# Output projection of the scan stage: half rows of 256 columns over eight e-tiles in place of whole rows over four

## The reference

```python
def _L3_cond_ref(x, c, ...):              # S=512, D=512, E=1024, N=16, R=64
    def _ssm(u, Wdbc, Wdt, bdt, Alog, Dp):
        dlt, Bm, Cm = split(u @ Wdbc.T)
        delta = softplus(dlt @ Wdt.T + bdt)
        dA, dBu = exp(delta * A), delta * Bm * u
        h = dA_t * h + dBu_t              # a scan over time, for each e and each of N=16 states
        y = sum_n h * C_t
        return y + u * Dp
    z1 = _ssm(mz @ Wc1.T + bc1, ...)                  # first direction
    z2 = flip(_ssm(flip(mz @ Wc2.T + bc2), ...))      # second direction
    out = einsum('bse,de->bsd', act_mx * z1 + act_mx * z2, Wf) + bf + skip
    return x + gate[:, None, :] * out
```

## Time and profile before

| | us |
|---|---|
| median of 3 runs | 6557.69 |
| lowest, highest | 6544.21, 6568.91 |
| profiled execution | 6555.72 |
| its span | 6553.9 |
| the scan stage in it | from about 3450 to the end |

### The profile page before, as it was taken

One profiled execution on the slowest core, in us unless ns is written; L12 is line 12 of the kernel. 1 busy time (PEld: TensorE's weight loads), 2 busy tenths in 40 slices (PEclk: granted clock), 3 DMA queues, 4 the chain that ended last, 5 costly groups with the idle time before them and its releaser, 6 DMA issues. The chain is left out here.

```text
span 6553.9 us, 129603 instructions
## 1 busy us (share of the span) xinstructions
PE 5787.2 (88%) x54624; PEld 3049.2 (47%) x54624; DVE 4470.7 (68%) x6093; ACT 2749.7 (42%) x4645; POOL 2867.4 (44%) x921
## 2 busy tenths in 40 slices
PE   8899979996878777885988999999999999999998
PEld 2455545553444444442444545555454554545454
DVE  1265545554555565556628989989898998989886
ACT  0022212222333333331116666666566665656564
POOL 0010000000000000002326888888788887878886
PEclk9999989998988888887999999999999999999999
DMA  5200010101000000002431111111011111111110
GB/s 197 73 29 29 21 69 29 36 20 62 15 16 15 1 15 15 7 7 80 151 138 47 52 60 50 58 53 54 30 50 61 50 58 52 49 36 50 60 40 26
DMA packets 143104, 321.75 MB, mean 49 GB/s; under 512 B 25786, under 2 KB 27195, under 8 KB 132299
## 3 DMA queue, kind: packets, MB, share of 16 engines
q1 hardware_dynamic: 142546, 313.72, 13.9%
HBM read 238.79 MB, written 74.89 MB: 48 GB/s over the span
## 5 line engine op out<-in xcount | busy, mean ns | idle before, releaser
L1379 POOL TENSOR_TENSOR sc_state<-sc_state,sc_c_rows 128x2048 f32<-128x2048 f32 x512 | 2327.0, 4552 | 515.9 <-DVE sc_state L1663 512.3
L1663 DVE TENSOR_TENSOR_SCAN sc_state<-sc_decay,wide 128x512 f32<-128x512 f32 x2048 | 2342.9, 1202 | 285.6 <-PE wide L1533 285.3
L1462 ACT ACTIVATE sc_decay<-sc_delta,sc_neg_a 128x512 f32<-128x512 f32 x2048 | 1431.7, 717 | 1000.7 <-DVE sc_state L1663 1000.7
L1533 PEld LDWEIGHTS wide<-sc_diag,sc_du_t 64*64 64x64 f32 x32768 | 934.2, 133 | 682.0 <-DVE sc_state L1663 377.1
L1550 PE MATMUL wide<-sc_state,sc_half 64*64 64x512 f32 x8192 | 1080.6, 607 | 152.2 <-issue 140.7
L1533 PE MATMUL wide<-sc_diag,sc_du_t 64*64 64x128 f32 x32768 | 1123.1, 274 | 29.6 <-DVE sc_state L1663 25.6
L639 POOL TENSOR_SCALAR l_y_rstd<-l_y_mv 128x4 f32<-128x4 f32 x24 | 5.6, 234 | 1511.6 <-DVE l_y_mv L805 1511.6
L520 ACT ACTIVATE l_prob<-l_prob,l_s_max 128x512 f32<-128x512 f32 x512 | 363.2, 710 | 722.1 <-DVE l_s_max L536 722.0
L484 PE MATMUL wide<-l_ident,l_prob 128*128 128x128 f32 x2048 | 374.7, 338 | 266.7 <-DVE l_prob_t L553 266.3
L460 PE MATMUL wide<-l_w,l_xn_t 128*128 128x512 f32 x1280 | 556.3, 592 | 2.1 <-PEq L84 2.1
L1507 PE MATMUL wide<-sc_xn_t,sc_w_z 128*128 128x512 f32 x1024 | 508.9, 620 | 0.0
(11 more groups left out here) (171 smaller groups left out, 5953.4 us busy)
## 6 DMA issues: line engine op xcount, KB each, us to landing
sc_c_rows<-c_d SPq DMA_DIRECT2D x64, 1024.0 KB, 4.8
sc_w_z<-wz_tiles SPq DMA_DIRECT2D x128, 256.0 KB, 2.7
x<-l_out SPq DMA_DIRECT2D x24, 1024.0 KB, 4.9
l_x<-x SPq DMA_DIRECT2D x16, 1024.0 KB, 7.1
mx_d<-fr_mx SPq DMA_DIRECT2D x16, 1024.0 KB, 4.2
sc_mx<-mx_d SPq DMA_DIRECT2D x64, 256.0 KB, 2.6
pro_w_mod<-in_mod_w SPq DMA_DIRECT2D x6, 2048.0 KB, 8.4
l_w<-in_att_w SPq DMA_DIRECT2D x12, 1024.0 KB, 13.2
```

The source lines that it names most:

```text
L1379: pool.tensor_tensor(state[quad % STATES][:, :, :], state[quad % STATES][:, :, :], c_rows[(r * 4 + q) % ROWS][:, :, :], ALU.mult).then_inc ...
L1462: act.activation(decay[step % DECAYS][:, :], delta[slot % 2][:, :], ACT.Exp, scale=neg_a[:, s, m, n:n + 1]).then_inc(decay_ready, 1)
L1533: last = pe.matmul(to[cols_to, k, :, :], du_t[slot % 2][rows, k, cols_to], diag[rows, c, k, :, :], start=True, stop=True)
L1663: dve.tensor_tensor_scan(state[quad % STATES][:, step % 4, order], decay[step % DECAYS][:, order], pair[:, i, order], 0.0, ALU.mult, ALU.a ...
```

## The change

A row of 128 x 512 is made as two pieces of 128 x 256, each with all eight k, in the left half of `z_bank`. Piece 0 to 7 of a sequence are made in the slots at place 1 to 8, so in seven e-tiles of the first direction and the first of the second. Each of these slots has eight matmuls (two in each of the chunks 4 to 7) of 256 columns. VectorE drains each piece by itself into its half of `o_gated`, at places 2 to 9. GpSimd adds the residual once per row as before, at places 3, 5, 7 and 9 in place of 2 to 5. SyncE stores at places 4, 6, 8 and 10 in place of 3 to 6. `o_full` and `o_drained` count pieces now.

```diff
-                    if q == 1 and s == 0 and b >= 1 and 2 <= m <= 5:
-                        output(b - 1, m - 2)
+                    if q == 1 and b >= 1 and slot % 16 in (3, 5, 7, 9):
+                        output(b - 1, (slot % 16 - 3) // 2)
...
-                        if s == 0 and b >= 1 and m >= 3:
-                            pe.wait_ge(o_drained, (b - 1) * TT + min(m - 2, TT))
+                        if b >= 1 and slot % 16 >= 3:
+                            pe.wait_ge(o_drained, (b - 1) * 2 * TT + min(slot % 16 - 2, 2 * TT))
...
-                def output(b, t, ks):
+                def output(b, piece, ks):
+                    t, h = piece // 2, piece % 2
                     if 0 in ks:
                         pe.wait_ge(gated_ready, (b + 1) * ET)
-                        pe.wait_ge(o_drained, b * TT + t)
+                        pe.wait_ge(o_drained, b * 2 * TT + piece)
                     for k in ks:
-                        last = pe.matmul(z_bank, gated[:, k, t * P:(t + 1) * P], w_out[:, k, :],
-                                         start=(k == 0), stop=(k == ET - 1))
+                        last = pe.matmul(z_bank[:, 0:256], gated[:, k, t * P:(t + 1) * P],
+                                         w_out[:, k, h * 256:(h + 1) * 256], start=(k == 0), stop=(k == ET - 1))
...
-                    if 1 <= b < B and s == 0 and 1 <= m <= 4 and c >= 4:
+                    if 1 <= b < B and 1 <= slot % 16 <= 8 and c >= 4:
...
-                for t in range(TT):
-                    output(B - 1, t, range(ET))
+                for piece in range(2 * TT):
+                    output(B - 1, piece, range(ET))
...
-                    dve.tensor_tensor(o_gated[:, :], z_bank, gate[:, :], ALU.mult).then_inc(o_drained, 1)
+                    dve.tensor_tensor(o_gated[:, h], z_bank[:, 0:256], gate[:, h], ALU.mult).then_inc(o_drained, 1)
...
-                    if c == 0 and b >= 1 and s == 0 and 2 <= m <= 5:
-                        output(b - 1, m - 2)
+                    if c == 0 and b >= 1 and 2 <= slot % 16 <= 9:
+                        output(b - 1, slot % 16 - 2)
```

More of the change, by code:

```diff
@@ L1303, in _ @@
                         load_xn(b + 1)
-                    if s == 0 and b >= 1:
-                        o = b - 1
-                        if m == 0:
+                    if b >= 1:
+                        o, at = b - 1, slot % 16
+                        if at == 0:
                             load_gate(o)
[L1308 to L1319, removed]
+                        if at in (4, 6, 8, 10):
+                            store(o, at // 2 - 2)
+                        if at in (0, 2, 4, 6):
+                            t = at // 2
+                            if o * TT + t >= 2:
+                                sp.wait_ge(out_stored[t % 2], (o * 2 + t // 2) * 16)
+                            load_resid(o, t)
                     if m == 7 and r + 1 < 2 * B:
@@ L1323, in _ @@
                             load_c(4 * (r + 1) + q)
-                sp.wait_ge(o_drained, (B - 1) * TT)
+                sp.wait_ge(o_drained, (B - 1) * 2 * TT)
                 load_gate(B - 1)
@@ L1358, in gating @@
                     if m == 0 and b >= 1:
-                        pool.wait_ge(o_full, b * TT)
+                        pool.wait_ge(o_full, b * 2 * TT)
                     pool.tensor_tensor(gated[:, m, :], y_sum[:, m, :], mx[m % 2][:, :], ALU.mult
@@ L1363, in output @@
                 def output(b, t):
-                    pool.wait_ge(o_drained, b * TT + t + 1)
+                    pool.wait_ge(o_drained, 2 * (b * TT + t + 1))
                     pool.wait_ge(resid_loaded[t % 2], (b * 2 + t // 2 + 1) * 16)
@@ L1593, in _ @@
                             pe.wait_ge(z_direct, slot + 2)
-                        output(b - 1, m - 1, range(2 * c - 8, 2 * c - 6))
-                for t in range(TT):
-                    output(B - 1, t, range(ET))
+                        output(b - 1, slot % 16 - 1, range(2 * c - 8, 2 * c - 6))
+                for piece in range(2 * TT):
+                    output(B - 1, piece, range(ET))
             @block.vector
@@ L1642, in add_swapped, with output @@
                     dve.tensor_tensor(y_sum[:, m, :], s_bank, y_sum[:, m, :], ALU.add).then_inc(y_added, 1)
-                def output(b, t):
-                    if t == 0:
+                def output(b, piece):
+                    t, h = piece // 2, slice(piece % 2 * 256, (piece % 2 + 1) * 256)
+                    if piece == 0:
                         dve.wait_ge(gate_loaded, (b + 1) * 16)
-                    dve.wait_ge(o_full, b * TT + t + 1)
+                    dve.wait_ge(o_full, b * 2 * TT + piece + 1)
                     if b * TT + t >= 1:
                         dve.wait_ge(out_ready, b * TT + t)
-                    dve.tensor_tensor(o_gated[:, :], z_bank, gate[:, :], ALU.mult).then_inc(o_drained, 1)
+                    dve.tensor_tensor(o_gated[:, h], z_bank[:, 0:256], gate[:, h], ALU.mult).then_inc(o_drained, 1)
                 def scans(chunk):
@@ L1680, in _ @@
                         add_swapped(slot - 1)
-                    if c == 0 and b >= 1 and s == 0 and 2 <= m <= 5:
-                        output(b - 1, m - 2)
+                    if c == 0 and b >= 1 and 2 <= slot % 16 <= 9:
+                        output(b - 1, slot % 16 - 2)
                 add_sums(SLOTS - 1)
                 add_swapped(SLOTS - 1)
-                for t in range(TT):
-                    output(B - 1, t)
+                for piece in range(2 * TT):
+                    output(B - 1, piece)
 def program(nc, d, out):
```

## The result

| | before | after |
|---|---|---|
| median, us | 6553.46 (20 runs) | 6578.50 (20 runs) |
| lowest to highest | 6525.22 to 6575.27 | 6562.47 to 6592.03 |
| profiled execution, its span | 6555.72, 6553.9 | 6589.83, 6587.9 |

Ratio 1.0044, 95% interval 1.0031 to 1.0057: slower by 25 us by the medians and 29 by the ratio, close to what was forecast (6577), and within the 0.5% that was called no change. The interval goes from 20 to 37 us, so the ratio alone can't test the terms of the sum.

What follows compares the result with a forecast made beforehand. PE bounds the scan stage; output work costs PE time in full beyond a free 3.41 us behind `turn`. From 6555.72: +25.7 loop, +2.2 end, -6.8 clock, or +21.1, gives 6577 us, range 6553 to 6606.

Steps and rivals of the forecast that it cites:

- Part 1 and 2: PE at places 1 to 8: slots of 25.58 us, eight taking 204.98 against 201.31; +25.7 us over seven sequences.
- The switch of 0.36 us: PE going from quarters to full array and back, paid per chunk with output work in chunks 5 to 7: 0.36 us.
- the line and both bounds: Other estimates for a 256-column PE instruction: 0.225 us on a straight line between bounds of 0.120 and 0.435.
- the room behind `turn`: Stretch from `turn` to the first `sums`: fixed length, PE work in it free up to about 3.4 us.
- The 0.14 us "absorbed somewhere": In slots with output before: costs summed to 28.30 us, 28.14 was measured; the difference was also taken off the new slot.
- Part 3: End of the program: a row as two pieces takes 8.54 us against 7.98, +2.2 us for four rows.
- Parts 4 and 5: VectorE's added drains (+0.5 us a sequence) and GpSimd's and SyncE's moved additions and stores: cost nothing.
- Part 6: Half-clock stretches in second-direction slots: two places a sequence now carry output, so four stretches of 1.70 us fewer, -6.8 us.
- A: Rival: PE's gaps in eight slots swallow work and switches, 23.93 us a slot, 6489 us in all; chance 0.05.
- B: Rival: the clock falls in slots with output work, idle before chunk 5's `sums`: +25 us, 6602; chance 0.15.
- C: Rival: GpSimd becomes late at place 7 and PE waits 2.3 us a sequence: +16 us, 6593; chance 0.08.
- D: Rival: PE weight loads stand open behind short matmuls, 60 us in the loop and 14 at the end: 6652; chance 0.02.

Runs made afterwards that it cites:

- filled pair: Kernel before and changed kernel, each with unread 512-column matmuls behind `turn` in second-direction gaps without output work: medians 6525.64 and 6555.45 us.
- first filled kernel: Kernel before plus two unread 512-column matmuls behind `turn` in second-direction slots, from place 8 on: ratio 0.9969.
- narrow kernel: Kernel before with rows made as two 256-column halves in the same four slots: ratio 1.0023, or 0.9974 with unread matmuls in second-direction gaps.

## Why the prediction was right

- *Part 1 and 2, the loop.* 25.58 us a slot and 204.98 for the eight were forecast; 25.58 and 205.00 are in the trace, and the filled pair gives 26.4 us for the loop against 25.7. The switch of 0.36 us was worked out as a remainder and has since been measured alone (26.30 - 25.58 = 2 x 0.36). The 0.2155 us of a 256-column instruction is the 0.215 taken, and the 0.225 of the line and both bounds weren't needed. That the room behind `turn` doesn't move is seen in the 3.42 us; of it PE idled 0.77 us, a little less than the 0.8 to 1.0 forecast. The 0.14 us "absorbed somewhere" was carried over from the kernel before without a reason, and it held: of the three bare chunks only the first two take 1.74 and 1.73 us, and the third takes 4376.84 - 4374.99 = 1.85, so there output work adds 0.12 us less than the sum had.
- *Part 3, the end.* 8.60 us a row, 8.54 forecast: +2.5 by the rows at full clock and by the filled pair's traces, 2.2 forecast. VectorE's 256 columns took 0.42 us there (0.41).
- *Parts 4 and 5.* VectorE, GpSimd and SyncE cost nothing visible, as taken. SyncE's loads of the residual rows moved too, to places 0, 2, 4 and 6 in place of 0, 1, 3 and 4, which the prediction didn't weigh; no slot is longer for it.
- *Part 6, the clock, had no ground.* I took off 6.8 us because two susceptible slots a sequence now carry output. Those slots were indeed spared, but stretches came in others: 16 in the profile against 17, so 1.7 us in this pair, and single profiles scatter from 3 to 29. Filling the gap took 0.34% from the kernel before and 0.31% from the changed one, 22 and 20 us, so the credit is 2 us by this, with intervals that hold both 0 and 6.8. The unfilled means of 20 runs each, 6550.7 and 6579.8, differ by 29.1, with some 8 us either way, and don't decide it either. It also named the places 8 and 9; the two that count are 7 and 8, as the first filled kernel showed.
- The forecast of 6577 is nearer to 6578.5 than its working deserves: the profiled execution from which it started lay 2.3 us above the median of 20 runs, and it took off 6.8 us of clock where the two profiles differ by 1.7. With neither it would have been 6553.5 + 27.9 = 6581.4, which is inside the runs' scatter too. So the match to 1.5 us is in part luck; that of the slots is not.
- *Rivals.* A (gaps swallow the work) is excluded by the chunk of 2.95 us; the experiment with all matmuls in chunk 4 shows what it would have needed, work put where the gap is. B (the clock falls in slots with output) didn't come in any profile of the series. C and D are excluded by GpSimd's timeline and by the narrow kernel: its 448 added loads of the full array cost 0.9 us in the loop, and only the first step of a run is longer. The Trainium skill ("TensorE: Matmul & The Clock Gate", section "The mechanism") says that a weight load overlaps running matmuls only in other rows of the array; by that sentence alone the added loads would have stood open, and they didn't. The same section of the Trainium skill also has loads pulled ahead when they go to the background weight buffer. The prediction passed over this, and the 0.9 us agree with it.

What stays open: why some gaps of 1.44 us are followed by a half-clock stretch and others aren't. Slots at places 0 to 6 have the same gap of 1.44 us, with 0.12 us of idle ahead in place of 0.29, and had none. The prediction's range was right, but its assumption on the number of stretches had no mechanism behind it.

## What to carry to other kernels

Spreading work over more steps to fill idle time pays only if it is put where the idle time is: here the same instructions cost 205 us for eight slots spread over four chunks and 192 in one. Before you split a run of matmuls, subtract a bare step from one that holds the run; what its columns don't explain is paid again with each new run. And where PE must wait anyway, free work in the gap can be worth its place for the clock alone: here 0.3%.

## What was not expected

- The half-clock stretches come in rows. A slot that has one lasts 23.93 us in place of 22.23, and in the unfilled profiles most are followed by one in the next slot, up to eight in one sequence. The number in the loop went from 17 to 29 between profiles of kernels with output slots of 28.14 and 28.17 us, and from 16 to 3 between 25.58 and 25.56.
- An execution is so regular that its slots repeat to 0.01 us; most of the scatter between runs, up to 80 us, goes with the clock. In the 20 runs of the changed kernel span and mean granted clock have a correlation of -0.97, and with the gap filled seven runs of the kernel before lay within 8 us where 26 unfilled ones beside them lay within 36.
